# Two staging tiles instead of one for the decay tiles that ScalarE writes to scratch

## The reference

```python
# attention, x is (8, 2048, 1024), H = 16 heads of 64
x = x + attn(layernorm(x))
#   q = rope(h @ wq.T); k = rope(h @ wk.T); v = h @ wv.T
#   scores = q k^T / 8 + slope[h] * (kpos - qpos), causal
#   out = softmax(scores) v;  out @ out_w.T + out_b
# feed-forward
x = x + ffn(layernorm(x))
#   y = per-rail 16x16 products, z = per-rail 16->64 products, 4 heads
#   gelu(z), 16384 wide, @ w_cproj.T
```

## Time and profile before

| what | us |
|---|---|
| median of the runs shown | 4171.06 |
| its two runs | 4143.68 and 4198.44 |
| the profiled execution | 4153.95 |
| span of its slowest core (core 1) | 4152.4 |
| spans of the other cores | 4096.4 to 4150.5 |

### The profile page before, as it was taken

The page is one execution under the profiler, slowest core; times in us unless marked ns, Lnnn a source line. Parts: engine busy times, 40 slices in busy tenths (PEclk is TensorE's granted clock), DMA queues, the critical chain, the costliest instruction groups (busy, mean ns, idle before and its releaser), DMA issues.

```text
span 4152.4 us, 33118 instructions; the slowest of 8 cores (4096.4 to 4152.4 us)
## 1 busy us (share of the span) xinstructions
PE 2401.6 (58%) x7966; PEld 838.3 (20%) x7966; DVE 691.0 (17%) x1547; ACT 1055.5 (25%) x1967; POOL 253.1 (6%) x481
## 2 busy tenths in 40 slices
PE   1286000352000000089999997996789789889889
PEld 0032000010000000012222221222234334334334
DVE  3202820002000000044444443221000000000000
ACT  2222022100000000045555553112533233233320
POOL 0011000113111111100000000000000000000000
PEclk9977555555555555555555555555799999999999
DMA  1212011456444454400000001222589889888889
GB/s 41 51 21 36 0 38 48 68 77 97 93 93 92 89 95 93 92 27 20 13 13 9 11 13 31 74 76 64 172 261 271 254 264 272 254 263 274 263 268 286
DMA packets 346071, 475.18 MB, mean 114 GB/s; under 512 B 58144, under 2 KB 193312, under 8 KB 345888
## 3 DMA queue, kind: packets, MB, share of 16 engines
q1 hardware_dynamic: 257024, 375.50, 30.1%
q0 software_dynamic: 65824, 61.90, 11.3%
q10 hardware_dynamic: 23040, 35.66, 2.3%
HBM read 465.57 MB, written 69.21 MB: 129 GB/s over the span
## 4 chain that ended last, share of the span: by engine, by line
PE 43%; DMA 35%; DVE 7%; issue 6%; ACT 6%; SPq 2%; POOL 1%; DVEq 0%; ACTq 0%; POOLq 0%
PE pf L1041 14%; DMA wcs<-wcb 11%; DMA wcv<-wcT 10%; PE po L747 7%; PE ps L671 6%; DMA wcb<-wcv 6%; PE pat L896 5%; DMA dscr<-dstage 4%; PE pqk L382 3%; DMA wqb<-wvT 3%; PE pc L797 2%; PE pf L991 2%; PE pqk L507 1%; DMA bbuf<-blkB 1%; ACT dstage L482 1%
## 5 line engine op out<-in xcount | busy, mean ns | idle before, releaser
L1041 PE MATMUL pf<-wcs,Hb 128*128 128x512 bf16 x4096 | 1006.8, 383 | 160.3 <-DMA wcs<-wcb 157.6
L671 PE MATMUL ps<-QT,KT 64*128 64x512 bf16 x559 | 336.6, 604 | 732.0 <-ACT ebuf L705 731.3
L1004 ACT ACTIVATE Hb<-pf 128x256 bf16<-128x256 f32 x1024 | 393.3, 384 | 735.1 <-PE pf L991 708.2
L1041 PEld LDWEIGHTS pf<-wcs,Hb 128*128 128x128 bf16 x4096 | 391.8, 98 | 590.4 <-issue 231.8
L705 ACT ACTIVATE ebuf<-ps,cpool 128x1024 bf16<-128x1024 f32 x128 | 142.6, 1114 | 1005.4 <-DMA dfar<-dscr 823.3
L747 PE MATMUL po<-pbuf,Vx 128*65 128x512 bf16 x559 | 353.4, 634 | 42.9 <-DVE Ost L806 42.0
L507 PE MATMUL pqk<-wqb,At 128*128 128x512 bf16 x256 | 119.3, 610 | 447.2 <-ACT Vx L520 353.3
L991 PE MATMUL pf<-btb,w2b 128*128 128x256 bf16 x1024 | 287.8, 288 | 40.3 <-issue 14.6
L671 PEld LDWEIGHTS ps<-QT,KT 64*128 64x128 bf16 x559 | 55.7, 100 | 1025.8 <-issue 1025.8
L725 DVE TENSOR_TENSOR pbuf<-ebuf,ddg 128x512 bf16<-128x512 bf16 x256 | 108.8, 425 | 913.4 <-ACT ebuf L705 899.7
L712 ACT ACTIVATE ebuf<-ps,cpool 128x512 bf16<-128x512 f32 x303 | 208.2, 687 | 144.2 <-PE ps L671 119.3
(11 more groups left out here) (91 smaller groups left out, 1074.5 us busy)
## 6 DMA issues: line engine op xcount, KB each, us to landing
wcs<-wcb SPq DMA_DIRECT2D x1024, 256.0 KB, 5.3
wcv<-wcT POOLq DMA_DIRECT2D x256, 128.0 KB, 3.2
wcb<-wcv SPq DMA_DIRECT2D x256, 128.0 KB, 1.7
w2b<-w2scr SPq DMA_DIRECT2D x256, 128.0 KB, 3.8
wqb<-wvT POOLq DMA_DIRECT2D x64, 256.0 KB, 4.1
dscr<-dstage ACTq DMA_DIRECT2D x80, 128.0 KB, 1.9
xin<-x SPq DMA_DIRECT2D x16, 512.0 KB, 4.3
ddg<-dscr SPq DMA_DIRECT2D x64, 128.0 KB, 2.3
```

The costliest lines, as they stand in the source:

```text
L671: P.op("tensor", (lambda p_=pr, f_=hf, kc_=kc, hb_=hb, hc_=hc, qc_=qc: (lambda e: e.matmul(ps[p_][:, 512 * f_:512 * (f_ + 1)], KT[hb_:hb_ ...
L1004: P.op("scalar", (lambda m_=mc, z_=zb, p_=p: (lambda e: e.activation(Hb2[p_][:, SB2 * m_:SB2 * (m_ + 1)], pf[z_][:, 0:SB2], AF.Gelu, bias= ...
L1041: P.op("tensor", (lambda m_=mc, s_=sl2, e_=e2, pi=pb_i, i_=i, p_=p: (lambda e: e.matmul(pf[pi][:], Hb2[p_][:, SB2 * m_ + 128 * s_:SB2 * m_ ...
```

## The change

`dstage` becomes two tiles that take turns by a counter `k5`. Each has a semaphore of its own for the landing of its store (`dds0`, `dds1`), and an exponential waits for the store of its own tile, the one two tiles earlier. `ev_dscr`, for which the loads of the decay tiles wait, becomes the pair of both final values. Nothing is moved in the order of any engine's list.

```diff
-    dstage = p2_es.enter_context(nc.sbuf_tensor("dstage", [128, 512], BF16, side="right"))
+    dstage = [p2_es.enter_context(nc.sbuf_tensor(f"dstage{i}", [128, 512], BF16, side="right"))
+              for i in range(2)]
...
-    dst_free = None
+    dst_free = [None, None]
+    k5 = 0
     for h in range(NH):
         sh = slope(h)
         for t5 in range(5):
+            di = k5 % 2
+            k5 += 1
             xin_t = xfar if t5 == 4 else xdg[t5]
-            P.op("scalar", (lambda sh_=sh, x_=xin_t: (lambda e: e.activation(
-                dstage[:], x_[:], AF.Exp, bias=0.0, scale=sh_)))(),
-                 waits=[ev_gconst, dst_free], inc="s")
+            P.op("scalar", (lambda sh_=sh, x_=xin_t, i_=di: (lambda e: e.activation(
+                dstage[i_][:], x_[:], AF.Exp, bias=0.0, scale=sh_)))(),
+                 waits=[ev_gconst, dst_free[di]], inc="s")
             ev_dx = P.now("s")
-            P.op("scalar", (lambda h_=h, t_=t5: (lambda e: e.dma_start(
-                out=dscr_d[h_, t_], in_=dstage[:])))(),
-                 waits=[ev_dx], inc="dds")
-            dst_free = P.now("dds")
-    ev_dscr = P.now("dds")
+            P.op("scalar", (lambda h_=h, t_=t5, i_=di: (lambda e: e.dma_start(
+                out=dscr_d[h_, t_], in_=dstage[i_][:])))(),
+                 waits=[ev_dx], inc=f"dds{di}")
+            dst_free[di] = P.now(f"dds{di}")
+    ev_dscr = [P.now("dds0"), P.now("dds1")]
...
-                 waits=[ev_dscr, prev] if sf == 0 else (), inc=f"ddl{hp}")
+                 waits=ev_dscr + [prev] if sf == 0 else (), inc=f"ddl{hp}")
```

## The result

The changed kernel is faster by 2.4%: 4037.14 us (median of 11 runs) against 4126.52 us (10 runs), ratio 0.976 with a 95% interval of 0.972 to 0.980. The ratio leaves out the executions in which one die of the chip ran slower at a lower granted clock, the two medians do not, which is why their difference is smaller. The ratio means 98 us, interval 82 to 114; the forecast was 107 us, and 4047.

What follows compares the result with a forecast made beforehand. The prediction took the kernel to be bound from 541 to 756 us by ScalarE waiting for each store's landing, on a path without slack. 4153.95 - 107.2 + 0.3 = 4047 us, range 4022 to 4095.

Steps and rivals of the forecast that it cites:

- The place of the loss: Decay-tile loop, 541 to 756 us: ScalarE waits 164.3 us for store landings, on a path without slack.
- The price of a pair, L + 0.79: Loop with two tiles: issue-to-landing time L plus 0.79 us, 2.70 us per two tiles with L at 1.91.
- The landing with two in flight: Loop's stores: L taken as 1.91 us; the rival that landing grows to 2.3 to 2.9 had chance 0.12.
- the prediction's upper bounds: Loop's stores: landing at most 2.3 us (saving 92.4) or 2.9 us (saving 69.0).
- The argument from 0.38 us of engine time per store: Loop's stores: each occupies the DMA engines 0.38 us, so a second, 1.1 to 1.6 us later, finds them free.
- ScalarE's own limit: Loop: exponential, issue and the gaps take ScalarE 1.12 to 1.19 us per tile, below the landing's 1.35.
- The rule on memory load: Loop's stores: skill's rule that memory latency grows with load, 0.2 to 2 us, speaking against the change.
- The steps of the changed profile: Loop: store issues alternating about 1.15 and 1.55 us, waits near 36 us in every second tile.
- What is late next: First V eviction moves from 756.0 to 648.8; the Vx memsets, ending at 560.0, would be the next cover.
- The sum: Whole kernel: 107.2 us saved in the loop, 0.3 us added for semaphore waits, giving 4047 us.
- The level: Whole kernel: forecast starts from the profiled execution of 4153.95 us, 17 us below the median of runs shown.
- The other rivals: Behind the loop: gain given back in good part, 0.04; TensorE's clock changing, 0.02 slower, 0.01 faster.

Runs made afterwards that it cites:

- e3: Kernel before with one tile, only heads 0 to 7's decay tiles computed and stored, heads 8 to 15 loading those; ratio 0.9742 to the kernel before.
- e4: Kernel before with one tile, the loop moved in ScalarE's list behind the 32 stores of the folded rail tiles; ratio 0.9591 to the kernel before.
- e7: e4 with the changed kernel's two tiles and two semaphores; ratio 0.9588 to the kernel before.
- e6: e2 with the stores issued by SyncE's queue instead of ScalarE's; ratio 0.965 to the kernel before.
- e2: Changed kernel with four staging tiles and four semaphores instead of two; ratio 0.9711 to the kernel before.
- e8: e4 with VectorE's 16 memsets of Vx moved ahead of the sine and cosine tables; ratio 0.955 to the kernel before.
- e9: Changed kernel with the Vx memsets first and the 80 decay tiles spread between the V evictions; ratio 0.9516 to the kernel before, 3921 us.
- e1: The changed kernel again, no edit; ratio 0.9765 to the kernel before, 97 us of 4114 saved.
- e5: The kernel before again, no edit, for a second profile; ratio 0.998, spans 4079 to 4113 us.

## Why the prediction was right, point by point

**The place of the loss.** Right. The loop was on the path without slack: halving it (the change, e3) came off the end nearly whole, taking it off ScalarE's critical stretch (e4) took off more, and once it was covered its length no longer showed (e7).

**The price of a pair, L + 0.79.** Right. Measured 2.67 us for two tiles (105.3 / 39.5) against 2.70, and the loop 104 to 105 us against 106.8. The landing with two in flight, the one price that the trace didn't hold, had a median of 1.9 on six cores and 1.7 on two, as chosen or a little better. This size was a choice and not derived: beside other traffic the landings of such pairs had medians of 2.4 to 2.8 us (e7), inside the prediction's upper bounds. The argument from 0.38 us of engine time per store held too: the share doubled to 28.4% of half the time, and in e6 it rose to 51.9% with the median still at 1.7 on that core. ScalarE's own limit, worked out as 1.12 to 1.19, was 1.143 in e2.

**The rule on memory load.** The Trainium skill ("DMA: Bandwidth & Descriptors", "Latency and other measured facts") has latency grow with load. With nothing but these stores running, up to 178 GB/s for a core, the medians of the runs don't show it. Beside other transfers landings did grow: one tile beside the casts had medians of 2.0 to 2.2 us (e8), two tiles 2.4 to 2.8 beside the casts (e7) and 2.7 to 2.9 beside the V weights (e9). There the core moved less than in e6 (131 and 129 GB/s against 178), but its DMA engines were busier (0.61 and 0.70 against 0.52). So GB/s alone does not tell the landing; the runs don't separate the engines' busy share from the kind of transfer beside the stores.

The same page's section "Anatomy of one DMA" puts a small DMA's fixed time down to waiting for a confirmed write. That section is about DMAs that GpSimd issues, which the prediction did not say, and these stores were issued by ScalarE and SyncE. Their overlap fits that account (in e6 stores 0.74 us apart still landed 1.7 us after issue), but no run here shows what the time is spent on.

**The steps of the changed profile.** The wait was put at 36 us in every second tile, with steps of 1.15 and 1.55. The steps took turns as forecast, though less far apart (some 1.2 and 1.47 us on core 0 for most of the loop); on core 3 they came close to 1.33 each in the middle. The row of core 3 counts 54.6 us of waiting in 77 pieces and not 36 in 39. The pair was sized rightly; what was wrong was to take the short step for one without a wait for a landing. Nearly every exponential was released by a landing, also the short ones, and the row then counts the whole gap, including the 0.49 us of ScalarE's own issue, as waiting for the DMA.

**What is late next.** Right for the change, where the memsets ended 87 us before the loop did, and right as a bound: in e4 they held the first V eviction, at 545.8 on average.

**The sum.** The sign, the path and the pair were right; the size was somewhat too large. 107 us were forecast and 98 (82 to 114) measured, 97 (85 to 109) in e1. Two of the ten are a term that was a little too large: the loop taken from the profiled execution was 214 us, while in a second one it was 210 on average, because landings of 1.70 us occur as well; from 210 to 104.5 it is 105.5. The rest, some 8 us, could not be pinned to a stage. Taking the mean of the eight cores' spans in place of the slowest core, over the executions that enter the ratios, gives 98 us for e1 (91 to 104 by resampling, an estimate), 116 for e2 and 104 for e3, where the loops were shorter by 105, 120 and 110: each 4 to 7 less than the loop's shortening. One explanation is that in executions without a profile more cores had the 1.7 us landings, with which the shortening is 101 and not 109 (e5); no run shows it. The V stage is longer by 0.5 us, the casts by between -2 and +5, the feed-forward stage by between +1 and +12, and both of these vary as much between executions of one kernel. It may also be noise of the ratio, whose interval holds 107. e3, with half the stores and none overlapping, had no better ratio, so it is not the second tile. This stays open.

**The level.** 4047 was worked out from the profiled execution of 4153.95 us, which was 27 us above the median of all ten runs of before. That the loop started 15 us late on cores 0 and 1, and that die 0 took longer in the feed-forward stage, could have been seen by asking the other six cores; the prediction looked at core 0 alone, which was late itself. The gain that was forecast too large made up for a part, and 4047 came out 10 us above the measured median. That the level came so close is in part luck: two errors of opposite sign. The lower end of the range has a slip as well: 4028 less 10 is 4018 and not 4022, which changes nothing here.

**The other rivals.** Nothing was given back that can be shown; TensorE's clock was 0.50 in attention and 0.95 in the last stage as before. (The prediction's "0.50 in every stage" from 405 us on overlooks the V stage, whose row reads 0.53; 0.51 after.)

## What to carry to other kernels

An engine that waits for the landing of its own store before it refills one tile pays exponential, issue and landing in a row; two tiles cut that to the larger of half the round trip and the engine's own work, and the engine's own work includes the issue (here 0.33 us and the ways to and from it). Before more tiles, ask whether the loop has to stand where it does: moved into a stretch in which its engine waits anyway, the loop with one tile, even grown to 235 us, gave the better time than 105 us with two on the path (0.959 against 0.976). Then look at what its transfers meet there. What ends the next wait behind the loop bounds the gain (here 16 small memsets, 19 us behind its start), and the level of a forecast is only as good as the one execution that it was read from: compare cores before trusting it.

## What the runs showed of the hardware

The landing of a store of 128 KB from SBUF to DRAM had two levels with nothing else running: 1.70 and 1.90 us. In one execution of the kernel before (e5) core 6 was mostly at the lower and core 3 at the upper one, for the same instructions; in its first profile all cores were at 1.9. The number of stores in flight doesn't decide it: with one in flight six of eight cores had a median of 1.7 in e3, and with several the medians were 1.7 to 1.9 by core (e2, e6). What sets it was not found. It is worth up to 13 us of a loop of 80 waits (201.6 against 214.3 in e5).

Stores issued from one queue 0.74 us apart overlapped, at 178 GB/s from one core with all eight doing the same, and kept their median landing (e6). Beside GpSimd's weight loads it was 2.7 to 2.9 us, at 129 GB/s in all (e9).
